# A graph-attention layer's edge sort: both groups' k and v windows get a second buffer and are asked for a step ahead

## The reference, cut to what matters

```python
q = (embeds[rows] @ qW).reshape(e, HEADS, dh)
k = (embeds[cols] @ kW).reshape(e, HEADS, dh)
v = (embeds[cols] @ vW).reshape(e, HEADS, dh)
scores = jnp.clip(jnp.einsum('ehd,ehd->eh', q, k), -10.0, 10.0)
exp_s = jnp.exp(scores)
norms = jax.ops.segment_sum(exp_s, rows, num_segments=nvar)[rows]
w = exp_s / (norms + 1e-08)
res = jax.ops.segment_sum(w[:, :, None] * v, rows, num_segments=nvar).reshape(nvar, d)
...
x = _layernorm(x + _L0_gnn_ref(x, L0_gnn_qW, L0_gnn_kW, L0_gnn_vW, src, dst), axis=-1)
```

## Time and profile before

| | |
|---|---|
| median of 3 runs | 1709.44 us (1707.88 to 1710.03) |
| the profiled execution | 1711.48 us |
| its span, first to last instruction | 1709.3 us |
| mean granted TensorE clock | 0.936 of full |
| share of the span that PE / DVE / ACT / POOL was busy | 87% / 86% / 74% / 59% |

### The profile page before, as it was taken

How to read it: one execution, slowest core, us unless ns; L and a number is a source line. 1 busy time by engine, 2 the same in 40 slices (tenths; PEclk the granted TensorE clock), 3 DMA queues, 4 the chain that set the end, 5 groups by cost and what they waited for, 6 DMA issues and landing times.

```text
span 1709.3 us, 56067 instructions
## 1 busy us (share of the span) xinstructions
PE 1482.0 (87%) x19964; PEld 1425.5 (83%) x19965; DVE 1469.3 (86%) x2980; ACT 1265.3 (74%) x1844; POOL 1016.7 (59%) x764
## 2 busy tenths in 40 slices
PE   4873988888888988888769999999999999999990
PEld 3652878888788878887759999999999999999990
DVE  6988998898988998898158999999999999999987
ACT  2341665565666666665559999999999999999984
POOL 6230776777777776777725555555555555555551
PEclk8566999999999999999979999999999999999995
DMA  5673899999999999999897777777777777777732
GB/s 155 225 276 132 312 370 337 336 346 366 348 352 343 341 367 339 357 339 344 333 302 257 238 238 241 244 238 239 239 243 242 237 240 240 243 239 237 240 113 56
DMA packets 159451, 465.03 MB, mean 272 GB/s; under 512 B 36994, under 2 KB 59266, under 8 KB 152244
## 3 DMA queue, kind: packets, MB, share of 16 engines
q1 hardware_dynamic: 123572, 301.16, 54.1%
q0 software_dynamic: 35840, 163.36, 23.9%
HBM read 271.21 MB, written 209.73 MB: 281 GB/s over the span
## 4 chain that ended last, share of the span: by engine, by line
PE 80%; DVE 8%; issue 6%; DMA 2%; SPq 2%; ACT 1%; POOL 0%; DVEq 0%; POOLq 0%; ACTq 0%
PE two_a L1131 14%; PE two_b L1131 13%; PE meta L1193 12%; PE sum_bank L1193 12%; PE two_a L1214 7%; PE two_b L1214 7%; PE one_d L1204 3%; PE one_c L1204 3%; PE meta L1149 2%; PE one_d L1160 2%; DMA work<-kv_table 1%; PE sum_bank L1113 1%; SPq L825 1%; DVE acc L1614 1%; DVE cols_work L1315 1%
## 5 line engine op out<-in xcount | busy, mean ns | idle before, releaser
L698 POOL TENSOR_TENSOR work<-work 128x768 f32<-128x768 f32 x236 | 450.8, 1910 | 357.4 <-ACT work L939 357.4
L635 POOL DMA_INDIRECT sorted_rows<-work x448 | 501.3, 1119 | 215.2 <-issue 215.2
L948 ACT ACTIVATE work<-work 128x1024 f32<-128x1024 bf16 x236 | 500.8, 2122 | 0.0
L1131 PE MATMUL two_a<-work 128*128 128x192 bf16 x2688 | 268.5, 251 | 86.8 <-issue 84.3
L903 ACT ACTIVATE work<-two_a 128x768 f32<-128x768 f32 x224 | 181.5, 810 | 187.0 <-PE two_a L1131 186.2
L1131 PEld LDWEIGHTS two_a<-work 128*128 128x128 f16 x2688 | 220.0, 100 | 107.5 <-issue 89.0
L1131 PE MATMUL two_b<-work 128*128 128x192 bf16 x2688 | 267.5, 251 | 0.0
L1193 PE MATMUL meta<-work 128*128 128x100 f32 x1888 | 236.1, 278 | 0.8 <-DVE acc L1548 0.8
L1193 PE MATMUL sum_bank<-work 128*128 128x100 f32 x1888 | 235.2, 278 | 0.0
L1579 DVE TENSOR_REDUCE work<-work 128x32 f32<-128x768 f32 x236 | 225.0, 953 | 8.2
L1131 PEld LDWEIGHTS two_b<-work 128*128 128x128 f16 x2688 | 225.9, 100 | 6.8
(11 more groups left out here) (229 smaller groups left out, 2211.8 us busy)
## 6 DMA issues: line engine op xcount, KB each, us to landing
work<-sorted_rows SPq DMA_DIRECT2D x472, 392.0 KB, 3.5
work<-sorted_local SPq DMA_DIRECT2D x56, 1024.0 KB
sorted_rows<-pad_rows SPq DMA_DIRECT2D x49, 392.0 KB, 4.5
work<-kv_table SPq DMA_DIRECT2D x112, 144.0 KB
sorted_rows<-work POOLq DMA_INDIRECT x448
kv_table<-work SPq DMA_DIRECT2D x12, 576.0 KB, 3.4
work<-in_x SPq DMA_DIRECT2D x12, 192.0 KB, 3.8
sorted_local<-work SPq DMA_DIRECT2D x56, 8.0 KB
```

The source lines that it names most:

```text
L635: pool.indirect_dma_start(out=rows_dram, out_offset=bass.IndirectOffsetOnAxis(ap=place_now[:, p, u, b:b + 1], axis=0), in_=payload[:, p, u ...
L698: pool.tensor_tensor(now[:, :, 0:D].rearrange("p c (h f) -> p c h f", h=HEADS), blk[:, k, :, :, D:2 * D].rearrange("p m c (h f) -> p (m c) ...
L948: act.activation(hot_f[:, k % HOTF], hot[:, k % HOTS].rearrange("p n c -> p c n"), ACT.Copy).then_inc(hotf_made[k % PSEM], 1)
L1131: mm = pe.matmul(to, picked[:, u % 2, k * P:(k + 1) * P], window[:, u, :, n, :], start=(n == 0), stop=(n == 2))
```

## The change

The window buffer gets a leading dimension of 2: steps of even and odd number use different halves. SP loads both windows of step c+1 together. It does so at the very start of its part of step c, ahead of the places, as soon as both `kv` of step c−1 are done with that half (`back=1` in `group_done`). The semaphores `window_in` now count by half and no longer by group, and PE waits once per step, before `kv(0)`, for both windows. The bytes moved, the number of DMAs and all instructions on the other engines are as before.

```diff
-        WORK = 28360
+        WORK = 28936
...
-        window, at = share(at, [QUAD, 2, 3, D], BF16)
+        window, at = share(at, [2, QUAD, 2, 3, D], BF16)
...
-        window_in = sems("window_in", QUAD)
+        window_in = sems("window_in", 2)
...
-            def window_of(u, lo, at_c):
-                group_done(sp, kv_made[KPARTS - 1], u, at_c)
-                sp.dma_start(window[:, u].rearrange("p x a b -> p (x a b)"), kv3[bass.ds(lo, P), :]
-                             ).then_inc(window_in[u], 16)
+            def windows(los, p):
+                for u in range(QUAD):
+                    sp.dma_start(window[:, p, u].rearrange("p x a b -> p (x a b)"), kv3[bass.ds(los[u], P), :]
+                                 ).then_inc(window_in[p], 16)
 
             def emit(a, b, c, p=None):
-                following = c is None or not isinstance(c, int) or c + 1 < NQ
                 if c is None and b == 1:
-                    los = bases(0)
+                    windows(bases(0), 0)
+                if c is not None and (not isinstance(c, int) or c + 1 < NQ):
+
+                    p = parity(c, p)
+                    los, at_c = bases(plus(sp, c, 1)), counts(sp, c, G2, 0)
                     for u in range(QUAD):
-                        window_of(u, los[u], {})
-                if c is not None and following:
-                    c1 = plus(sp, c, 1)
-                    los, at_c = bases(c1), counts(sp, c, G2, 1)
+                        group_done(sp, kv_made[KPARTS - 1], u, at_c, 1)
+                    sp.sem_inc(sp_turn, 1)
+                    windows(los, 1 - p)
                 if b is not None:
                     half = bass.ds(low_bits(sp, b, 1), 1)
                     sp.wait_ge(local_rows_made, plus(sp, b, 1))
...
-                if c is not None and following:
-                    window_of(0, los[0], at_c)
                 if b is not None:
 
                     sp.wait_ge(local_out, times(sp, b, 16, 16))
...
-                if c is not None and following:
-                    for u in range(1, QUAD):
-                        window_of(u, los[u], at_c)
...
-                    done_c, c16 = counts(pe, c, G2, 1 - G2), times(pe, c, 16, 16)
+                    p = parity(c, p)
+
+                    done_c, loaded = counts(pe, c, G2, 1 - G2), times(pe, c, 8 * QUAD, 8 * QUAD * (2 - p))
...
-                    pe.wait_ge(window_in[u], c16)
+                    if u == 0:
+                        pe.wait_ge(window_in[p], loaded)
```

More of the change, by code:

```diff
@@ L1130, in kv @@
                         for n in range(3):
-                            mm = pe.matmul(to, picked[:, u % 2, k * P:(k + 1) * P], window[:, u, :, n, :],
+                            mm = pe.matmul(to, picked[:, u % 2, k * P:(k + 1) * P], window[:, p, u, :, n, :],
                                            start=(n == 0), stop=(n == 2))
```

## The result

The changed kernel takes 1732.53 us (median of 4 runs, 1730.92 to 1733.86), the kernel before 1709.22 us beside it (4 runs, 1707.88 to 1710.03). The ratio is 1.0137, 95% interval 1.0119 to 1.0154: slower by 1.4%, 46 us above the forecast of 1687 and outside its range of 1667 to 1706. The profiled execution of the changed kernel took 1732.3 us, its span 1730.2 us.

A forecast was written before the change was run, and what follows sets the result against it. PE's wait for the window of `kv(1)` was taken to bound each sorting step: 12.31 to 11.85 us, 53 × 0.46 = 24 us, less 1 for the end; 1709.44 − 23 = 1686.4, forecast 1687 us, range 1667 to 1706.

The forecast's parts named there:

- What bounds the kernel: Sorting phase: a closed loop of `kv(1)` 4.05 us, issue 0.33 us and window load bounds every step, 12.31 us.
- L: Time from asking for the window of `kv(1)` until it is there, put at 7.9 us from the 12.31 us step.
- The second buffer and the earlier request: Both windows asked for a step ahead, there after some 9 us with 3 us to spare; their loop bounds nothing.
- Removed: PE's 1.61 us a step: PE's idle time before `kv(1)`, 1.61 us a step, goes as a wait for the window.
- SP's queue: Places issued no later, landing up to 0.8 us later behind the extra 144 KB; cost 0 while `brow` has slack.
- The signs: What would show the forecast right (no idle before `kv(1)`, share 0.98, phase end near 835 us) or wrong.
- Slower: `brow` comes too late: Rival: `brow` behind two windows holds its reader if landing takes over 15.9 us; 1751 at 17.5 us; slower 0.08 in all.
- The DMA engines have no more to give: Rival: the long-run DMA rate stays at some 360 GB/s, steps take 11.9 to 12.0 us, 1691 us; chance 0.18.
- The sum: Sorting phase: 0.46 us a step over 53 steps is 24 us, less 1 us at the end: 23 us gained.

The follow-up runs named there:

- x6: Changed kernel with both windows asked for behind the places, ahead of the wait for them: 1695.27 us (one run), kernel before 1708.05 us beside it.
- m3: SP's DMAs and POOL's scatters only, sorting work of PE, DVE, ACT left out, request orders varied: 12.1 (before), 12.7 (changed), 10.5 (windows behind places), 13.0 (changed), 11.2 (before) us a step.
- r9: Changed kernel with both windows asked for behind the places, ahead of the wait for them: 2002.91 us, kernel before 2039.19 us beside it.
- r1: Changed kernel with both windows asked for behind the places, ahead of the wait for them: 2004.24 us, kernel before 2014.45 us, ratio 0.9979.
- m2: Sorting work of PE, DVE and ACT left out, scatters held back until all `brow` are there: 5.82 us a step in the changed kernel's request order.

## Why the prediction was wrong

*What bounds the kernel* was right. I had named the window by exclusion; the trace's semaphore events bear it out: the windows landed at 711.09, 723.48 and 735.10, each 0.09 us before its `kv(1)`. The loop closes on the rows, 5.61 + 0.33 + 6.45 = 12.39 us and 4.05 + 0.33 + 7.24 = 11.62. So L is not 7.9 in the mean: part of the 12.31 is the lower clock in `kv(1)`. With the double buffer and an order that leaves SP's loop short (x6) a step falls to 11.95 us. How much of that is the buffer and how much the order isn't known, since x6 differs from the kernel before in both.

*The second buffer and the earlier request.* "Removed: PE's 1.61 us a step" was right for `kv(1)`. But "both windows of step c+1 are now asked for at the end of `kv(1)` of step c−1" holds for the first steps only. That is the earliest moment; the real one is when SP comes to it, behind the wait for the places and behind `brow`. From the eighth step on that is later, and the wait is back at `kv(0)`, 59.4 us in 32 waits.

*SP's queue* is the step that failed: "They land up to 0.8 us later behind the extra 144 KB … Cost: 0 while `brow` has slack". I costed a delay of one transfer and asked if the reader had slack. I should have gone round SP's own loop: `brow`, 3.0 us, places, 10.3 us, `brow`, that is 12.5 to 13.4 us, more than the 11.85 that I wanted a step to take. The size was wrong too: in m3 the windows ahead of the places land 2.5 to 2.7 us behind `brow` in the order of before (one window) and 4.2 to 4.4 us in the changed one (two). The extra 144 KB cost 1.5 to 1.9 us there, not 0.8, and they cost it at each turn of the loop. The rows were there: before the change `brow` goes out at 711.84 and at 724.35, 12.5 us apart, and SP waits up to 2.8 us for the places. I used them for `brow`'s reader only; the queue-alone run shows that the order of before, driven by nothing but the queue, takes 11.2 to 12.1 us. By that the loop had 0.2 to 1.1 us to spare in a step of 12.31, and the change adds 0.6 to 2.

How it builds up is seen in the first steps. At 180.22 the places leave 7.25 us behind `brow` and are there 4.05 us later; at 254.69 they leave 3.03 us behind it and need 10.34. The closer the places come behind `brow`, the later they land, and the next `brow` goes out later still, until SP has no free time. From there each step is the loop's.

*The signs.* Two of the signs of being wrong came: PE idle before `kv(0)` for its windows, and DVE waiting for `brow`. Of the signs of being right came the pairs of windows and a `kv(1)` without idle time; the share of 0.98, the fewer stretches at the lower clock and the end near 835 us did not.

*The rivals.* "Slower: `brow` comes too late" had the right queue and the wrong price. It asked for 15.9 us from `brow`'s issue to its landing, which "would need transfers far slower than any that the rows show". `brow` need not be slow: in the changed kernel it lands 8.3 us behind its issue in the mean. DVE does wait for it, 29.3 us, since it is asked for late. What decides is the landing of the 8 KB behind it, on which SP waits, and that asks only for a loop of over 12.31 us. "The DMA engines have no more to give" and its 11.9 to 12.0 us a step look right in x6 (358 GB/s, 11.95 us), and the Trainium skill, DMA: Bandwidth & Descriptors, Specifications, has about 358 GB/s for a core; but 415 GB/s over 94.5 us in m3 shows that neither is a hard limit, and x6's waits are for scatters. POOL is as near: 8 × (1.139 + 0.30) = 11.5 us a step, worked out from 436.2 us for 383 scatters in x6. Which of them holds x6 at 11.95 wasn't tried.

*The sum.* 23 us were forecast for the gain; x6 has 12.8 against the one run beside it. Its profiled execution is 16.2 us below that of the kernel before (1711.48), and 14.9 of these are in the sorting phase (last scatter at 841.02, before at 855.91). They add up so. The first steps gained too, for PE waited for windows there as well, 8.0 us in five waits: the tenth sort starts at 248.97 before and at 246.06 in x6, 2.9 us earlier. The 46 steps from there to the last sort take 12.31 us before and 12.00 in x6, where 11.85 was forecast: 14.4 us. The end gives 2.5 us back: the last scatter is issued 42.9 us behind the start of the last sort, and 40.5 before, where I had taken off 1 us. The change as made is 23 us above the kernel before: its phase ends 19.8 us later (875.67).

```profile
855.91 0.97 POOL L635 DMA_INDIRECT sorted_rows<-work  x1 [0.30 <-issue]
```

```profile
875.67 0.97 POOL L635 DMA_INDIRECT sorted_rows<-work  x1 [0.31 <-issue]
```

```profile
841.02 0.97 POOL L635 DMA_INDIRECT sorted_rows<-work  x1 [0.30 <-issue]
```

(The three rows are the last scatter of the kernel before, the changed kernel and x6.) What is shown is that the place of the two window requests in SP's order makes the difference between 1732.5 and 1695.3 us: nothing else differs between the changed kernel and x6, and the chips of the two differ by 1 us in the kernel before (1709.2 and 1708.05). x6 is a single run. That the lower clock is a consequence is read from PE's timeline and from x6's 1.00; it wasn't tried by itself.

## What to carry to other kernels

Moving a request "earlier" on an in-order queue only makes it early if the queue's own loop is shorter than the step: walk that loop, each issue, each wait and what the awaited transfer has ahead of it, and do it with the step time that the change aims at. A small transfer that something waits for belongs ahead of the big ones, and big loads that are needed a step later belong behind it, inside its waiting time: here that order was worth 37 us. If a wait in the order of work stands ahead of a request, the request's time is that of the wait, whatever the buffers allow.

## What the runs showed of the hardware

The same program, the kernel before, took 1708 to 1712 us on some chips and 1966 to 2039 us (medians) on others. The record gives the chips of r9 and x6 the same number, 11, and the kernel before took 2039 us beside the one and 1708 beside the other. So it isn't shown that the kind is a property of the chip. All of the difference is in the sorting phase (in r1 the last scatter is issued at 1153 us, and from there to the end it is 852 us, before 853), where the engines wait for "remote" (rows of r1): a PE matmul that ended long before is seen late by DVE and ACT, for instance by DVE at 519.07 for the one that starts at 514.87 and takes 0.21 us. By the trace's semaphore events in r1 the delay from the end of a PE matmul to its count is 1.3 us in the mean in this phase; it is 0.01 us in the kernel before on a chip like the first. Why it differs stays open. Versions that differ by 37 us on the one kind of chip don't differ reliably on the other, so the first thing to read in a comparison is what the kernel before took beside it.

The share of the DMA engines is no measure of room: 0.98 and 361 GB/s, then 1.02 and 415 GB/s, in one run with the same transfers in another order. And 8 KB took 3.1 us with nothing else under way (the changed kernel at 169.92), 10.3 us behind 1.3 MB with scatters beside it (at 254.69), and 3.6 us behind the same 1.3 MB without scatters (m2).
